# Token mixer of an audio tower on one core: head products of the queries turned, sums of squares on TensorE, orders rewritten

## What is computed

```
conv  = conv1d(x, kernel[9, 64, 128])              # valid, 367 steps
v     = conv * where(wnorm < 1, 1, 1 / (wnorm + 1e-7))   # wnorm: root of the windowed sum of squares of x
h     = relu(tanh(|v|) * sign(v) + bias)
h    += layernorm-attention(layernorm(h))          # one score matrix, softmax in three bands (24, 168, 180), mean of the three
# the expert layer, on hn = layernorm(h):
q     = (hn @ Wq.T + bq) as 8 heads x 64
q     = (q - mean) / sqrt(var + 1e-5) * ln_g + ln_b         # per head
s0,s1 = l2norm(q[:32]) @ l2norm(keys0).T, l2norm(q[32:]) @ l2norm(keys1).T   # 2 x 64 scores per head
top 16 of each, top 16 of the 16 x 16 sums, softmax, expert = ix0 + ix1
out   = sum over heads and picks of  w * gelu(hn . down[expert]) * up[expert]
h    += out
```

## Time and profile before

| | us |
|---|---|
| median of 3 runs | 1392.88 (1389.09 to 1393.25) |
| profiled execution | 1389.55 |
| its span, first to last instruction | 1387.7 |
| VectorE busy | 1284.9 (93%) |
| TensorE busy | 1029.8 (74%) |
| GpSimd busy | 940.4 (68%) |
| ScalarE busy | 919.2 (66%) |
| chain that ended last, VectorE's share | 60% and 15% "issue" |

### The profile page before, as it was taken

The page is one execution under the profiler, slowest core; times in us unless marked ns, Lnnn a source line. Parts: engine busy times, 40 slices in busy tenths (PEclk is TensorE's granted clock), DMA queues, the critical chain, the costliest instruction groups (busy, mean ns, idle before and its releaser), DMA issues.

```text
span 1387.7 us, 41186 instructions
## 1 busy us (share of the span) xinstructions
PE 1029.8 (74%) x9585; PEld 679.4 (49%) x9585; DVE 1284.9 (93%) x10050; ACT 919.2 (66%) x4155; POOL 940.4 (68%) x1947
## 2 busy tenths in 40 slices
PE   4767777877777777778778777786778878776753
PEld 2434554645455454555446454553545545463433
DVE  4349999999999989999899998999999999999995
ACT  2576867668586857858576784767658676766532
POOL 4438776786867768577677867676776777668552
PEclk7787786769788776878877696787868778685555
DMA  2100000000000000000000000000000000000000
GB/s 55 18 15 2 3 11 3 4 8 6 10 4 11 4 5 11 4 10 4 12 4 5 9 6 10 4 12 3 5 9 5 6 3 5 4 4 5 3 4 7
DMA packets 22512, 10.97 MB, mean 8 GB/s; under 512 B 13920, under 2 KB 22032, under 8 KB 22242
## 3 DMA queue, kind: packets, MB, share of 16 engines
q1 hardware_dynamic: 21618, 7.79, 2.5%
q10 hardware_dynamic: 624, 0.30, 0.1%
HBM read 4.58 MB, written 3.01 MB: 5 GB/s over the span
## 4 chain that ended last, share of the span: by engine, by line
DVE 60%; issue 15%; PE 8%; ACT 7%; POOL 6%; SPq 1%; DVEq 1%; DMA 0%; POOLq 0%; ACTq 0%
DVE idx L1466 14%; DVE val L1464 9%; DVE cr L1536 8%; DVE scores L1469 8%; DVE oh L1479 6%; DVE best L1534 4%; DVE wl L1499 3%; ACT ns_junk L863 2%; PE banks L1055 2%; DVE bns L1389 2%; DVE masked L1419 1%; POOL cs L623 1%; PE bankM L1219 1%; PE bankQ L1142 1%; ACT act_g L840 1%
## 5 line engine op out<-in xcount | busy, mean ns | idle before, releaser
L1466 DVE FIND_INDEX8 idx<-val,scores 124x8 uint16<-124x64 f32 x1536 | 304.4, 216 | 0.0
L1464 DVE MAX8 val<-scores 124x8 f32<-124x64 f32 x1536 | 210.6, 207 | 2.4 <-ACT scores L870 1.2
L1219 PE MATMUL bankM<-wl,oh 128*128 128x16 f16 x5952 | 162.8, 172 | 46.2 <-DVE wl L1499 46.2
L1219 PEld LDWEIGHTS bankM<-wl,oh 128*128 128x128 f16 x5952 | 160.0, 101 | 59.6 <-DVE wl L1499 33.2
L597 POOL TENSOR_TENSOR qscale<-nmx,power 124x16 f32<-124x16 f32 x48 | 147.8, 3079 | 45.4 <-DVE nmx L1443 45.3
L1469 DVE MATCH_REPLACE8 scores<-val,scores 124x64 f32<-124x64 f32 x768 | 151.4, 206 | 0.0
L863 ACT ACTIVATE ns_junk<-bankQ 124x32 f32<-124x32 f32 x768 | 138.0, 255 | 12.7 <-PE bankQ L1172 12.4
L1479 DVE TENSOR_SCALAR oh<-eh 128x992 f16<-128x992 int16 x384 | 135.2, 414 | 4.5 <-ACT eh L918 4.5
L863 ACT ACTIVATION_READ_ACCUMULATOR ns_junk<-bankQ 124x1 f32 x768 | 138.3, 268 | 0.0
L1108 PE MATMUL banks<-diag,probs 124*124 124x124 f32 x672 | 107.7, 327 | 25.0 <-ACT diag L808 25.0
L1227 PE MATMUL bankM<-up_x,prod 128*124 128x128 f32 x384 | 86.5, 396 | 50.5 <-DVE prod L1508 50.5
(11 more groups left out here) (196 smaller groups left out, 3067.8 us busy)
## 6 DMA issues: line engine op xcount, KB each, us to landing
x_in<-in_x SPq DMA_DIRECT2D x16, 93.8 KB
x_in<-in_x SPq DMA_DIRECT2D x16, 62.5 KB
out<-o_sb SPq DMA_DIRECT2D x16, 62.0 KB
out<-o_sb SPq DMA_DIRECT2D x16, 61.0 KB
out<-o_sb SPq DMA_DIRECT2D x16, 60.5 KB
x_in<-in_x SPq DMA_DIRECT2D x16, 31.0 KB
oh<-more SPq DMA_DIRECT2D x6, 54.0 KB
conv_w<-in_L_tok_kernel ACTq DMA_DIRECT2D x2, 128.0 KB, 3.2
```

Source lines behind the costliest of these rows:

```text
L1219: last = e.matmul(coef[:, g, :, :], oh[:, k, g, :, :].rearrange("p v t -> p (v t)"), wl[:, part, k, :, TG * g:TG * (g + 1)], start=k + par ...
L1464: last = v.max(out=v_[:, hd, s, best8], in_=src[:, hd, s, :])
L1466: last = v.max_index(out=i_[:, hd, s, best8], in_max=v_[:, hd, s, best8], in_values=src[:, hd, s, :])
```

## The change

The two products of the queries are turned: the weights are the stationary operand, four blocks of 128 columns, two heads a block (`PAIRS` = 4), and hn is the moving one, so that the 64 values of a head lie on partitions. Each product is now four groups of a float32 matmul of 124 columns and a bfloat16 one. ScalarE squares all 4 x 124 columns with one activation into `sqT`, and TensorE sums over the partitions with a constant `blocks_sb` of ones (2 columns for whole heads, 4 for half heads) as the moving operand. The result lies in `bankQ` with positions on the partitions: one small activation adds 1e-5 and copies it to `qvar` (`q_var`), and VectorE's `q_guard` reads the half-head sums from PSUM. `bankQ` is free only when `nmx` is made, so `q_inner` and the next `q_product` wait on `nmx_ready`, a semaphore of VectorE. One more small DMA loads `blocks_sb`, and it counts in `ffn_in`.

```diff
@@ loads
-                     (own_sb[:, :], own), (merge_sb[:, :], merge)]
+                     (own_sb[:, :], own), (blocks_sb[:, :], blocks), (merge_sb[:, :], merge)]
@@ POOL q_std
-                pool.wait_ge(qss_ready, n + 1)
+                pool.wait_ge(qvar_ready, n + 1)
-                link(g.tensor_tensor(qvar[:, :], qss[:, :], eps8[:, :], ALU.add))
@@ ACT
-                wait(act, std_ready, 5 * n - 4)
-                for i in range(H):
-                    last = a.activation(sq_junk[:, i, :], bankQ[0:NT, i * QD:(i + 1) * QD], ACT.Square, scale=QD ** -0.5, accum_out=qss[:, i:i + 1])
-                last.then_inc(qss_ready, 1)
+                a.activation(sqT[:, :], bankQ[:, 0:PAIRS * NT], ACT.Square, scale=QD ** -0.5).then_inc(squared, 1)
+
+            def q_var(c, t):
+                act.wait_ge(qsum_done, n + 1)
+                wait(act, std_ready, 4 * n)
+                a.activation(qvar[:, :], bankQ[0:NT, 0:H], ACT.Identity, bias=eps8[:, 0:1]).then_inc(qvar_ready, 1)
...
-                wait(act, nmx_ready, n)
-                for i in range(2 * H):
-                    last = a.activation(ns_junk[:, i, :], bankQ[0:NT, i * HALF:(i + 1) * HALF], ACT.Square, accum_out=nss[:, i // 2, i % 2:i % 2 + 1])
-                last.then_inc(nss_ready, 1)
+                a.activation(sqT[:, :], bankQ[:, 0:PAIRS * NT], ACT.Square).then_inc(squared2, 1)
@@ PE q_inner, q_product
-                    pe.wait_ge(nss_ready, 3 * b + 1)
+                    pe.wait_ge(nmx_ready, 3 * b + 1)
...
-                wait(pe, nss_ready, n)
+                wait(pe, nmx_ready, n)
...
-                e.matmul(bankQ[0:NT, :], hnT[c.par][:, t, :], fwqT[:, :], start=True, stop=False)
-                e.matmul(bankQ[0:NT, :], ones3[:, :], fbq3[:, :], start=False, stop=True).then_inc(q_done, 1)
+                for k in range(PAIRS):
+                    e.matmul(bankQ[:, k * NT:(k + 1) * NT], fwqT[:, k * 128:(k + 1) * 128], hnT[c.par][:, t, :], start=True, stop=False)
+                    last = e.matmul(bankQ[:, k * NT:(k + 1) * NT], fbq3[:, k * 128:(k + 1) * 128], ones3[:, :], start=False, stop=True)
+                last.then_inc(q_done, 1)
+
+            def q_sums(c, t):
+                pe.wait_ge(squared, n + 1)
+                for k in range(PAIRS):
+                    last = e.matmul(bankQ[0:NT, 2 * k:2 * k + 2], sqT[:, k * NT:(k + 1) * NT], blocks_sb[:, 0:2], start=True, stop=True)
+                last.then_inc(qsum_done, 1)
@@ PE q_second turned in the same way; q_half_sums
+                pe.wait_ge(squared2, n + 1)
+                for k in range(PAIRS):
+                    last = e.matmul(bankQ[0:NT, 4 * k:4 * k + 4], sqT[:, k * NT:(k + 1) * NT], blocks_sb[:, 2:6], start=True, stop=True)
+                last.then_inc(nss_ready, 1)
@@ PE body
                 if at(c, 0):
                     key_products()
-                do(p1_conv, c + 1)
-                do(p1_sum_sq, c + 1)
                 if at(c, -1):
                     turn_weights()
+                do(turn_cells, c + -1, 0)
+                do(p1_conv, c + 1)
...
```

More of the change, by code:

```diff
@@ L67, in build @@
 def build(nc, x, tok_kernel, tok_bias, wq, bq, wk, bk, wo, bo, gamma, beta, fwq, fbq, lng, lnb,
-          keys0, keys1, down, up, merge, ident, own, out):
+          keys0, keys1, down, up, merge, ident, own, blocks, out):
     f32, f16, bf16, i16, u16 = mybir.dt.float32, mybir.dt.float16, mybir.dt.bfloat16, mybir.dt.int16, mybir.dt.uint16
@@ L283, in build @@
         q_done = sem("q_done")
-        qss_ready = sem("qss_ready")
+        squared = sem("squared")
+        qsum_done = sem("qsum_done")
+        qvar_ready = sem("qvar_ready")
+        squared2 = sem("squared2")
         std_ready = sem("std_ready")
@@ L1170, in q_second, with q_half_sums @@
                     pe.wait_ge(setup_act, 9)
-                e.matmul(bankQ[0:NT, :], hnT[c.par][:, t, :], wgT[:, :], start=True, stop=False)
-                e.matmul(bankQ[0:NT, :], std96T[:, :], bias96[:, 0:H * QD], start=False, stop=True).then_inc(q2_done, 1)
+                for k in range(PAIRS):
+                    e.matmul(bankQ[:, k * NT:(k + 1) * NT], wgT[:, k * 128:(k + 1) * 128], hnT[c.par][:, t, :], start=True, stop=False)
+                    last = e.matmul(bankQ[:, k * NT:(k + 1) * NT], bias96[:, k * 128:(k + 1) * 128], std96T[:, :], start=False, stop=True)
+                last.then_inc(q2_done, 1)
+            def q_half_sums(c, t):
+                n = c.tile(t)
+                pe.wait_ge(squared2, n + 1)
+                for k in range(PAIRS):
+                    last = e.matmul(bankQ[0:NT, 4 * k:4 * k + 4], sqT[:, k * NT:(k + 1) * NT], blocks_sb[:, 2:6], start=True, stop=True)
+                last.then_inc(nss_ready, 1)
             def q_score(c, t):
@@ L1551, in body @@
             def body(c):
+                if at(c, -1):
+                    key_norms()
+                do(invert_sums, c + -1, 0)
+                do(rank, c + -1, 1, 0, 0)
+                do(rank, c + -1, 1, 0, 1)
+                do(rank, c + -1, 1, 0, 2)
+                do(product, c + -2, 2)
                 do(p1_res, c)
-                do(product, c + -2, 2)
                 do(p1_stats, c, 1)
-                do(rank, c + -1, 1, 0, 2)
                 do(p1_moments, c, 1)
@@ L1594, in body @@
                 do(rank, c + -1, 2, 1, 2)
[L1595 to L1596 removed]
                 do(rank, c + -1, 2, 1, 3)
[L1598 to L1602 removed]
+                do(p1_smax, c + 1, 0)
                 do(choose, c + -1, 2, 0)
@@ L1607, in body @@
                 do(one_high, c + -1, 1, 0)
-                do(p1_smax, c + 1, 0)
                 do(one_low, c + -1, 1)
                 do(one_high, c + -1, 1, 1)
+                do(low_weights, c + -1, 1)
+                if at(c, 0):
+                    for step in range(4):
+                        rank(c, 0, 0, step)
+                do(sum_exps, c + -1, 2)
                 do(p1_rden, c + 1, 0)
-                do(low_weights, c + -1, 1)
                 do(p1_smax, c + 1, 1)
-                do(sum_exps, c + -1, 2)
+                do(invert_sums, c + -1, 2)
                 if not at(c, 0):
@@ L1617, in body @@
                     do(rank, c, 0, 0, 1)
+                if not at(c, 0):
+                    do(rank, c, 0, 0, 2)
+                do(product, c + -1, 1)
                 do(p1_rden, c + 1, 1)
-                do(invert_sums, c + -1, 2)
                 do(p1_smax, c + 1, 2)
+                if not at(c, 0):
+                    do(rank, c, 0, 0, 3)
                 if at(c, 0):
@@ L1668 @@
     given += [("merge", merge_matrix()), ("identity", np.eye(128, dtype=np.float32)),
-              ("own", np.tile(np.eye(TG, dtype=np.float32), (EH, 1)))]
+              ("own", np.tile(np.eye(TG, dtype=np.float32), (EH, 1))),
+              ("blocks", np.concatenate([np.kron(np.eye(k, dtype=np.float32), np.ones((128 // k, 1), np.float32)) for k in (2, 4)], 1))]
     for name, a in given:
```

188 lines of the change are left out of this document (92 added, 96 removed).

## The result

| | before | after |
|---|---|---|
| median of the runs, us | 1393.07 (1389.09 to 1394.31) | 1438.66 (1436.20 to 1440.67) |
| span of the profiled execution, us | 1387.7 | 1438.4 |
| ratio, with its 95% interval | | 1.0332 [1.0302, 1.0361] |

The forecast was 1398.0 us, from 1384 to 1411. The direction was right, the size was not: 45.6 us by the medians, 50.7 by the spans, where +7.2 had been summed.

The account below looks back on a forecast made before the run. VectorE was taken as the bound, 1284.9 us of work plus 102.8 idle. Terms 7.6 - 1.0 - 1.4 + 4.0 - 3.0 + 1.0 = +7.2 us gave 1396.8 or 1400.1; 1398.0 was named, range 1384 to 1411.

Parts of the forecast that it names:

- TensorE goes from about 63 to about 70 busy of 82 and hides that behind VectorE: Middle windows of 82 us: the new sums add 6.5 us a batch to TensorE, at no cost in time.
- the middle: Middle of the run: ScalarE is freer, so VectorE waits less for it; 3 us gained, between 0 and 7.
- the start: First convolution, now behind the turned expert weights: first `wsq` at 24.4 instead of 16.78, so 7.6 us late.
- the seam: Rival, first two loop-body steps: moving the loop cut could hide up to 16 us of issue waits, giving 1382; chance 0.15.
- I put the products at no change: Query products on TensorE: float32 part 1.04 us against 1.09 at full clock, 1.9 against 2.07 at 1.2 GHz.
- 0.135 us a pass: New sums on TensorE: price per pass from the `sq_win` row, 1.08 us a group of eight, 2.2 a tile.
- the rival that it costs nothing: Rival at the start: loads land early or the middle gives the loss back, so the old time, 1391; chance 0.18.
- The attention of batch 0: Start: ScalarE's copy and square of the next input go behind the last exponentials; 1.0 us gained, between 0 and 1.4.
- Gain 1.4: First query tile's chain, second product to `nmx`: 4.1 us instead of 5.5.
- The first MAX8: First ranking: some 9.5 us after `nmx`, behind a masked maximum; third `rden` 27.8 after; 4 us late, between 2 and 6.
- The second rival: Bank: `q_product` and `q_inner` wait for VectorE's `nmx`, delaying `smax`; 1.5 us for each of 14 batches, 1419; chance 0.12.
- `nmx` from PSUM costs 1 us: VectorE's `nmx` reads PSUM instead of SBUF: at most 0.1 us for each of 48, 1 us taken in all.

Follow-up runs that it names:

- runs 6: Changed kernel with the low half of the weights left out, 62 instead of 124 matmuls of each scatter, no query step touched: 1414.88 us, ratio 1.0178.
- run 4: Changed kernel with squares and block table in bfloat16, so each sum matmul is one pass instead of two: 1403.14 us, ratio 1.0075.
- 5: Changed kernel with every group of four sum matmuls issued twice: 1510.80 us, ratio 1.0862.
- run 13: `grouped_late_bf16`: changed kernel with each product's bias matmuls behind its float32 ones, weights turned after the first convolution's sum of squares, bfloat16 sums: 1389.64 us, ratio 0.9983.
- run 11: Changed kernel with bfloat16 squares and block table, and expert weights turned behind the first convolution's sum of squares: 1394.40 us, ratio 1.0033.
- Run 1: Changed kernel's new lists of all engines with the arithmetic of the kernel before, without the three new steps: 1419.74 us, ratio 1.0201.
- run 9: Changed kernel with the first product's bias table and its ones padded from 3 rows to 96, order of matmuls kept: 1424.25 us, ratio 1.0228.
- run 3: Changed kernel with the turning of the expert weights put behind the first convolution's sum of squares: 1431.33 us, ratio 1.0282.
- 2: New arithmetic in the lists of the kernel before, new steps entered one step behind what they wait for: 1532.47 us, ratio 1.1018.
- 7: Changed kernel with ScalarE copying the half sums to SBUF, so the next product waits for ScalarE, not VectorE: 1479.88 us, ratio 1.0628.

## Why the prediction was wrong

**The step that failed** is "TensorE goes from about 63 to about 70 busy of 82 and hides that behind VectorE". The number was right, 70.3, and the conclusion was not. It took TensorE's free 12 us as room. They are not free in a lump: in the kernel before TensorE waits in them for `prod` (50.5 us in the run), `wl` (46.2), GpSimd's `std` (33.9) and ScalarE's copies. That it is needed at once when these come is my reading; the runs show the price of its load, 0.30 to 0.61 us of time for each microsecond of busy time (runs 6, 4 and 5: 23.8/79, 35.5/83, 72.1/118.5; 0.27 to 0.62 by the ratios), and less as it comes near 65 of 82 (0.17 to 0.25, run 13 against run 11). The term "the middle", -3.0, measured +34. What it was reckoned from did come: VectorE's waits behind ScalarE fell by 17.5 us. Those behind TensorE, put at nothing, rose by 67.3.

**The lists** had been put at nothing outside the start and the seam. Run 1 says that this can't be taken for granted: with the old arithmetic they lose 19.5 us in the middle. With cheap sums the same lists lose 1.4 (run 4), so in the changed kernel the middle's loss hangs on the sums; how much of it other lists would save no run shows.

**"I put the products at no change"** failed as well. By elapsed time the first product has gone from 103 to 135 us over its 48 tiles, the second from 87 to 95. Scaling one row of 12 like passes by 8/12 counted passes and not the bias matmuls between them; 14.4 us of the run are the 3-row ones (run 9). "0.135 us a pass" was near at the full clock (0.93 us for eight, 0.116 each), and far from the estimate of 0.2 us a group by the floor in the Trainium skill (TensorE: Matmul & The Clock Gate, Part 1). But I priced both groups at that clock: 36 of the 48 first groups took 1.66 to 1.82 us, at or near 1.2 GHz (granted 0.50 to 0.54). So the sums measured 130.5 us of busy time, where 2.2 us a tile make 104.

**The start** held in its main term, and the rival that it costs nothing did not come. "24.4" for the first `wsq` was 24.49; 7.6 us was 7.3 in run 3. The attention of batch 0 gave 1.4 (third `rden` 50.49, against 44.17 + 7.7). "Gain 1.4" in the first query chain did not come, and `nmx` stood at 87.38, not at about 84.7. From the first product to the second it took 9.7 us, 1.0 more than before. From the second product to `nmx` it took 5.33 us, not 4.1: the timeline of the changed kernel has it at the lower clock, with 1.81 us for the sums.

```profile
82.05 0.79 PE L1187 MATMUL bankQ<-hnT,wgT 128*128 128x124 f32 x2 [0.37 <-ACT std96T L860]
...
85.52 1.81 PE L1196 MATMUL bankQ<-blocks_sb,sqT 128*124 128x4 f32 x8 [0.67 <-ACT sqT L866]
...
87.38 0.17 DVE L1474 TENSOR_TENSOR nmx<-bankQ,qguard 124x16 f32<-124x16 f32 x1 [4.59 <-PE bankQ L1196]
...
95.49 0.60 DVE L1495 MAX8 val<-scores 124x8 f32<-124x64 f32 x4
```

The first MAX8 came 8.1 us behind `nmx` (forecast 9.5), behind a masked maximum as written, and `rden` 27.3 (forecast 27.8). Up to 115 us the sum is 10.5 late, where 8.3 to 9.2 had been reckoned.

**The rivals.** The seam's premise came true, its issue waits fell from 16.0 to 2.3 us (one of its signs that the forecast was wrong), and the time did not: waits for TensorE took the place. `grouped_late_bf16`, which has the new seam and half of those waits (38.6 us), is 3 us under the kernel before. What the seam is worth by itself no run shows. The second rival named the symptom, a line of waits at `smax` in every batch, and 1.5 us a batch (31.4 us at `masked` are 2.0 a batch); I gave it the bank as its only cause and 0.12. A rival "TensorE's added work is late at VectorE, whatever it is" was missing, and it was the case.

What stays open: why each list suits only its own arithmetic (1, 2), the bank by itself (7), and what makes the 3-row matmuls slow (9). That `nmx` from PSUM costs 1 us was too small to be seen.

## What to carry to other kernels

Idle time of an in-order engine that every chain crosses is not room: before hiding work there, ask of each batch which waits of the full engine end on it, and don't price the added work at nothing; here it cost 0.3 to 0.6 of its busy time. A dose (the new work halved, then doubled) shows the price in two runs. When a product is cut into pieces, count the small matmuls between them, and keep a matmul of few rows out from between full ones, grouped at the end or padded.

## What the hardware showed that I had not expected

A bfloat16 matmul of 3 rows between float32 ones of 128 costs 0.23 us more at the full clock than one of 96 rows there (0.57 against 0.34 us a pair), though both show 0.22 us in their own record. And the eight float32 passes of a sum with 4 moving columns take 0.93 us where the four bfloat16 ones take 0.34: 0.116 and 0.085 us a pass.
